# Inverse roots by a power, another order of a pair, an ending by batches, and a second copy loaded early

## The reference

```python
x = x + _layernorm(_L0_attn_ref(_layernorm(x), wq, bq, wkv, bkv, wo))
x = x + _layernorm(_L0_ffn_ref(_layernorm(x), gate_w, w_gate, w_up, w_down, sh_gate, sh_up, sh_down))
```

```python
scores = softmax(x @ gate_w.T);  topk_w, topk_idx = top_k(scores, 6)
# of 64 experts each takes the first 64 of its tokens; later ones are dropped
d = (silu(buf @ w_gate) * (buf @ w_up)) @ w_down       # per expert, 256 -> 176 -> 256
y = sum over the 6 of topk_w * d  +  (silu(x @ sh_gate.T) * (x @ sh_up.T)) @ sh_down.T
```

## Time and profile before

| | us |
|---|---|
| median of three runs | 1533.69 (1531.11 to 1537.27) |
| the profiled execution, whole | 1528.5 |
| its span, first to last instruction | 1526.7 |
| attention stage, about | 20 to 1262 |
| norms, router and picks of batch 7 | 1262 to 1307 |
| experts, first matmul to last scatter's landing | 1330.6 to 1471.0 |
| ending | 1471.0 to 1526.7 |

### The profile page before, as it was taken

The page is one execution under the profiler, slowest core; times in us unless marked ns, Lnnn a source line. Parts: engine busy times, 40 slices in busy tenths (PEclk is TensorE's granted clock), DMA queues, the critical chain, the costliest instruction groups (busy, mean ns, idle before and its releaser), DMA issues. The chain is left out here.

```text
span 1526.7 us, 26086 instructions
## 1 busy us (share of the span) xinstructions
PE 1374.1 (90%) x8451; PEld 1175.1 (77%) x8451; DVE 1117.0 (73%) x3622; ACT 855.1 (56%) x2299; POOL 814.1 (53%) x1309
## 2 busy tenths in 40 slices
PE   4899999999999999999999999999999994499930
PEld 3788889888988898988888898889888983355510
DVE  4867686889687968887788778977887776444427
ACT  4666666566656665666666666665666651144414
POOL 2556565546555655475546555655555541355546
PEclk9799999999999999999999999999999996799965
DMA  7100000100010001000100010001000057199963
GB/s 271 56 1 1 14 15 8 32 22 15 8 32 22 15 1 39 22 15 2 39 22 15 1 39 22 15 1 39 22 15 1 25 163 230 49 280 300 291 191 161
DMA packets 49462, 95.89 MB, mean 63 GB/s; under 512 B 4177, under 2 KB 36402, under 8 KB 49330
## 3 DMA queue, kind: packets, MB, share of 16 engines
q1 hardware_dynamic: 43186, 84.80, 16.6%
q0 software_dynamic: 6144, 9.44, 3.1%
HBM read 67.74 MB, written 26.48 MB: 62 GB/s over the span
## 5 line engine op out<-in xcount | busy, mean ns | idle before, releaser
L1524 POOL TENSOR_TENSOR prob<-prob,rinv 128x512 f32<-128x512 f32 (+3 forms) x512 | 366.9, 724 | 205.7 <-DVE rinv L1184 203.7
L879 ACT ACTIVATE prob<-prob,negmax 128x512 f32<-128x512 f32 (+3 forms) x512 | 285.4, 558 | 86.7 <-DVE negmax L1177 85.9
L1511 POOL TENSOR_TENSOR q_l<-q_sum,q_h 128x128 fp32r<-128x128 f32 (+1 forms) x256 | 185.4, 745 | 144.2 <-ACT q_h L859 143.1
L529 PE MATMUL bank_o<-pt_h,v_h 128*128 128x128 f32 (+3 forms) x512 | 169.2, 330 | 0.0
L529 PE MATMUL bank_o<-pt_h,v_l 128*128 128x128 f32 (+3 forms) x512 | 165.4, 323 | 0.0
L529 PE MATMUL bank_o<-pt_l,v_h 128*128 128x128 f32 (+3 forms) x512 | 164.0, 320 | 0.0
L888 ACT ACTIVATE pt_h<-bank_s 128x128 fp32r<-128x128 f32 (+3 forms) x214 | 92.9, 434 | 77.5 <-PE bank_s L609 58.9
L859 ACT ACTIVATE q_h<-q_sum 128x512 fp32r<-128x512 f32 x128 | 80.2, 626 | 90.1 <-DVE q_sum L1154 90.1
L1177 DVE CUSTOM_DVE_ANT_0 prob<-bank_t,causal 128x384 f32<-128x384 f32 (+3 forms) x226 | 110.4, 488 | 23.8 <-PE bank_t L529 22.9
L1177 DVE CUSTOM_DVE_ANT_0 prob<-bank_s,causal 128x512 f32<-128x512 f32 (+3 forms) x217 | 107.9, 497 | 24.9 <-PE bank_s L529 24.1
L529 PE MATMUL bank_y<-o_h,wo_h 128*128 128x512 f32 x256 | 112.1, 438 | 5.5 <-DVE o_l L1195 5.5
(11 more groups left out here) (365 smaller groups left out, 4170.6 us busy)
## 6 DMA issues: line engine op xcount, KB each, us to landing
w_gu<-in_w_in SPq DMA_DIRECT2D x32, 704.0 KB
w_dn<-in_w_out SPq DMA_DIRECT2D x32, 352.0 KB
xio<-in_x SPq DMA_DIRECT2D x16, 512.0 KB, 3.9
token_table<-rows SPq DMA_DIRECT2D x8, 640.0 KB, 3.7
ffn_sums<-keys SPq DMA_DIRECT2D x4, 1024.0 KB
x_rows<-xio SPq DMA_DIRECT2D x8, 512.0 KB, 2.9
ffn_sums<-ytr SPq DMA_DIRECT2D x16, 256.0 KB, 2.1
fx<-x_rows SPq DMA_DIRECT2D x8, 512.0 KB, 9.3
```

Source lines behind the costliest of these rows:

```text
L529: return pe.matmul(o, l, r, start=start, stop=stop, skip_group_check=True)
L879: act.activation(p_, p_, ACT.Exp, bias=negmax[:, r, i:i + 1], scale=-1.0, accum_out=rsum[:, r, i:i + 1]).then_inc(exp_made, 1)
L1511: pool.tensor_tensor(l_[:, cols], q_sum[:, cols], plain(h_)[:, cols], ALU.subtract).then_inc(pos_low, 1)
L1524: pool.tensor_tensor(p_, p_, rinv[:, r, i:i + 1].to_broadcast([P, (i + 1) * P]), ALU.mult).then_inc(prob_made, 1)
```

## The change

- **Power.** `newton` and the guess go. GpSimd adds EPS to the variances and raises them to -0.5 in one `pow` instruction: `inverse_root`, two instructions for 128x4 numbers. `QUIET` has one step for each norm.
- **Order of a pair.** On TensorE: `expert_in` of the next pair, `activations_turn`, `expert_turn`, `add_second` of the pair before, `expert_out`. ScalarE's order follows.
- **Ending by batches.** Statistics, power, bias (now one VectorE instruction), normalising and residual go one batch at a time; the last batch in two halves.
- **Copies.** `TAIL = 3`: pairs 29, 30 and 31 add to copy 0. Copy 1 is complete with pair 27, and its eight loads are issued as soon as that has landed; copy 0 is loaded after all scatters.

```diff
+        COPY = [j % 2 for j in range(NP - TAIL)] + [0] * TAIL
+        def scattered(j):
+            return 16 * COPY[:j + 1].count(COPY[j])
...
-            for i in range(2):
-                sp.wait_ge(dma_s[i], 16 * (NP // 2))
-            for b in range(NB):
-                load_sums(b)
+            sp.wait_ge(dma_s[1], 16 * COPY.count(1))
+            for b in range(NB):
+                sp.wait_ge(down_in, min(NP, LASTUSE[b]))
+                sp.dma_start(fb[b][:], sum_runs[1][b]).then_inc(dma_f[b], 16)
+            sp.wait_ge(dma_s[0], 16 * COPY.count(0))
+            for b in range(NB):
+                sp.dma_start(fa[b][:], sum_runs[0][b]).then_inc(dma_f[b], 16)
...
             for j in range(NP):
+                if j + 1 < NP:
+                    expert_in(j + 1)
+                activations_turn(j)
                 if j + 2 < NP:
                     expert_turn(j + 2)
                 if j:
                     add_second(j - 1)
-                activations_turn(j)
-                if j + 1 < NP:
-                    expert_in(j + 1)
                 expert_out(j)
...
+            for b in range(NB):
+                add_sums(b)
+                if b:
+                    bias(b - 1)
+                variances(b)
+                if b:
+                    residual_out(b - 1)
+            bias(LAST)
+            residual_out(LAST, 2)
...
+            def inverse_root(mvt, nwt, n):
+                variances[0] += 1
+                pool.wait_ge(var_made, variances[0])
+                y = nwt[:, 0, 0:n]
+                done(pool.tensor_scalar(y, mvt[:, 0:n, 1:2].rearrange("p i o -> p (i o)"), EPS, None, ALU.add))
+                pool.tensor_tensor(y, y, minus_half[:, 0:n], ALU.pow).then_inc(inv_made, 1)
...
             def scatter(j):
                 if j > 1:
-                    pool.wait_ge(dma_s[j % 2], 16 * (j // 2))
+                    pool.wait_ge(dma_s[COPY[j]], scattered(j) - 16)
...
+            for b in range(NB):
+                add_sums(b)
+                inverse_root(fmv[b % 2], fnw[b], TT)
```

More of the change, by code:

```diff
@@ L18 @@
 EPS = 1e-5
-MAGIC = 0x5F3759DF
 BIG = 3.0e38
@@ L46, in build @@
     TRASH = 2 * CAP
+    TAIL = 3
     SUMROWS = NT + TRASH
@@ L139, in build @@
         mv = place("mv", [P, TT, 2], F32)
-        nw = place("nw", [P, 4, TT], F32)
+        nw = place("nw", [P, 1, TT], F32)
+        minus_half = place("minus_half", [P, TT], F32)
         zero_f = keys[:, CAP:CAP + ROW]
@@ L1050, in scalar_program @@
             for j in range(NP):
+                if j + 1 < NP:
+                    expert_act(j + 1)
+                activations_turn(j)
                 if j + 2 < NP:
@@ L1054, in scalar_program @@
                     first_out(j - 1)
-                activations_turn(j)
-                if j + 1 < NP:
-                    expert_act(j + 1)
                 expert_out(j)
@@ L1092, in variance @@
                     last = dve.bn_aggr(mvt[:, i, :], statt[:, i, :])
-                done(last)
-                v, y, a = (nwt[:, q, 0:n] for q in range(3))
-                done(dve.tensor_scalar(v, mvt[:, 0:n, 1:2].rearrange("p i o -> p (i o)"), EPS, None, ALU.add))
-                done(dve.tensor_scalar(a.bitcast(I32), v.bitcast(I32), 1, None, ALU.logical_shift_right))
-                dve.tensor_scalar(y.bitcast(I32), a.bitcast(I32), -1.0, float(MAGIC), ALU.mult, ALU.add
-                                  ).then_inc(var_made, 1)
+                last.then_inc(var_made, 1)
             VARS = [("x", 0)]
@@ L1490, in done @@
                 pool.wait_ge(pool_step, steps[0])
-            def newton(nwt, n, r):
-                v, y, a = (nwt[:, q, 0:n] for q in range(3))
-                if r == 0:
-                    variances[0] += 1
-                    pool.wait_ge(var_made, variances[0])
-                done(pool.tensor_tensor(a, y, y, ALU.mult))
-                done(pool.tensor_tensor(a, a, v, ALU.mult))
-                done(pool.tensor_scalar(a, a, -0.5, 1.5, ALU.mult, ALU.add))
-                last = pool.tensor_tensor(y, a, y, ALU.mult)
-                if r < 2:
-                    done(last)
-                else:
-                    last.then_inc(inv_made, 1)
             def position(l_, h_, step):
@@ L1557, in gpsimd_program @@
             pool.memset(zero_f, 0.0).then_inc(zero_made, 1)
-            for r in range(3):
-                newton(nw, TT, r)
+            done(pool.memset(minus_half[:], -0.5))
+            inverse_root(mv, nw, TT)
             pool.wait_ge(consts_made, 1)
@@ L1663, in _, with shape_constants @@
             tensor_program(e)
-def shape_constants(T, d, NT, cap):
+def shape_constants(T, d, NT, cap, pairs=32, last=3):
     import numpy as np
@@ L1678, in shape_constants @@
     keys = np.broadcast_to(-np.arange(half, dtype=np.float32), (d, half))
-    copy_of = (np.arange(d) // 2 % 2 * (NT + 2 * cap)).astype(np.float32)
+    pair = np.arange(d) // 2
+    copy_of = np.where(pair < pairs - last, pair % 2 * (NT + 2 * cap), 0).astype(np.float32)
     copy_at = np.stack([copy_of, copy_of + NT], axis=1).astype(np.float32)
```

103 lines of the change are left out of this document (41 added, 62 removed).

## The result

The changed kernel takes **1512.96 us** (median of 4 runs, 1510.01 to 1516.31) against 1532.4 us of the kernel before in the same comparison (1529.34 to 1537.27). The profiled run of after is the slowest of its four; its span is 1514.3 us, 12.4 less than before's 1526.7. The forecast counted in spans too, and had 1525.8.

The account below looks back on a forecast made before the run. It took TensorE to bound the attention stage and scatters most of the expert stage. Start -1.0, open norms -6.4, order 0, scatters +6.0, ending +0.5 gave -0.9: span 1525.8, median 1532.8 us, range 1522 to 1543.

Parts of the forecast that it names:

- The 21 norms beside the heads cost nothing and give nothing: Attention stage: TensorE busy 1079.20 of 1090.00 us, so shortening the norms there was counted as 0.
- The lock: Ending: VectorE and GpSimd instructions exclude each other, making a cycle 5.6 + p = 6.0 us a batch.
- Open norms: Two norms where other engines wait: from aggregate to normalising 0.80 instead of 4.00 us, saving 6.4 us.
- p: Time of GpSimd's one power instruction at a norm, taken as 0.4 us.
- The start: First norm of all: VectorE reaches the normalising 1.5 us sooner, of which 1.0 us was counted as saved.
- Rival B: Power is dear: ten times on the chain, each us above 0.4 costs 10; 1543.7 at p = 1.5; chance 0.15.
- F + 56.2: Ending: forecast end of the span, counted from F, the issue of copy 0's loads; before F + 55.7, so +0.5 us.
- Order of a pair: Expert stage: 3.8 us a pair on TensorE instead of 4.13, but scatters set the pace, so 0 counted.
- Serial scatters beside loads: Expert stage's tail: last scatters one behind the other, slowed by 4 MB of loads; last landing 1477.0 against 1471.0, +6.0 us.
- Rival A: Expert stage's tail: scatters not slowed by the loads, +0.4 in place of +6.0 us, total 1527.2; chance 0.18.
- The shorter load buys nothing: Ending: the chain of additions and statistics takes the place of the shorter load, +0.5 us.
- rival D: Ending: no lock between VectorE and GpSimd, cycle 4.4 us, six of them 9.6 less, total 1523.2; chance 0.12.

Follow-up runs that it names:

- e1_guess: Changed kernel with VectorE's three small guess steps put back at every norm but the ending's, results unused: 1516.18 us (0.990 of the kernel before).
- e5_newton: Changed kernel with eight of Newton's twelve small GpSimd steps put back, results unused, addition and power behind them: 1530.58 us (1.000 of the kernel before).
- e2_order: Changed kernel with the old order of a pair's pieces on TensorE and ScalarE: 1513.19 us (0.987 of the kernel before).
- e6_order: Kernel before with the power and the new order of a pair, nothing else of the change: 1492.58 us (0.975 of the kernel before).
- e8_ahead: Changed kernel with the ending's additions one batch ahead of the statistics and the bias on GpSimd: 1504.32 us (0.982 of the kernel before).
- e10_after: Changed kernel, unchanged, profiled once more: 1522.59 us.

## Why the prediction was wrong, step by step

The forecast of 1532.8 was 19.8 us too high. Of these, 11.5 lie in the spans (1525.8 forecast, 1514.3 measured). The other 8.3 come of which runs were profiled: that of before was 5.2 us below its median, which the forecast added, and that of after 3.4 above its own.

- **"The 21 norms beside the heads cost nothing and give nothing" failed.** It put at nothing what gave 19.2 us in the six batches alone, more than the whole 11.5; the middle of the expert stage hid a part of it. It was an argument from TensorE's busy time: 1079.20 of 1090.00 left 10.8 us. But busy time hid two things: the gaps are larger in the weight loads than in the matmuls (0.53 against 0.33 us at 370.45), and what counts is matmuls per us. The Trainium skill says in "Perfetto Trace Analysis", section "Identifying the Most-Contended Engine", that matmul busy time is no good measure of how near the limit TensorE is, and has one look at the busy share of weight loads and at what the matmuls compute instead. The trace agrees: busy time rose 1.0%, weight loads 1.9%, matmuls done 2.05%. The rows that should have been asked for are the waits of TensorE's weight loads: 15.3 us in six batches, each on a VectorE instruction. Experiments e1_guess and e5_newton show the norms' small steps to be their cause: VectorE's guess 0.9 us a batch, GpSimd's Newton the rest.
- **The lock was known and used in one place only.** Rows 10 gave it, in the form needed: the 1.68 us are those of a VectorE instruction with one tensor as input, as the normalising is. (The prediction set them beside a rule on instructions with two inputs; of its two rows only the 1.11 is of that kind.) The same row-by-row look at VectorE's normalising (516 and 614 ns in the middle, where the same form takes 399 at the least) would have shown VectorE losing some 2.4 us a batch.
- **Open norms: mechanism right, size off.** 2 x 2.53 = 5.1 us instead of 6.4, since p is 1.04, not 0.4. The small step of 0.20 was no guide to it. The start gave 1.4, of 1.0 forecast.
- **Rival B fell though its power was dear.** At p = 1.04 its rule gave 6.4 us more, of which 1.3 came, at the open norms. The ending's cycle came out at 6.06 all the same, since VectorE's addition (0.42) runs under the power, where the sum had put one behind the other. That F + 56.75 stood against F + 56.2 is therefore luck: a power taken too short and an addition that costs nothing cancelled. (The sum's last stretch, from GpSimd's start of batch 7 on, also makes 11.2 + p by its own terms, not 11.0 + p.)
- **Order of a pair: right for this kernel.** The scatters held (28 of 32 waited), and e2_order gives the same time. The reason reached too far: it denied a gain at the end of the stage too, and with alternating copies that is 3.6 us of tail (e6_order).
- **Serial scatters beside loads: +6.0 forecast, +5.1 in the profiles.** Within it pair 29 took longer and pair 30 less than forecast. Measured against what the new order allows (12.1) rather than against before (15.7), the tail costs 8.8 us in the profiles, 5.1 of it the loads'. Rival A falls.
- **"The shorter load buys nothing" held within 1.5 us** (56.75 against 58.1 and 58.25 with both copies loaded late), and so did the two-sided lock of the ending, but for VectorE's addition beside the power; rival D falls as a whole, though e8_ahead shows that 10 us lay in the order of the steps and the place of the bias. What the sum never asked was what the old closing would do with the power: 47.5 to 47.9 us, 9 less than the new one.
- **The middle of the expert stage, 0 forecast, +9.3 in the first profiles.** The forecast said "scatters in the middle still 8 to 9 us to landing" and TensorE's "share there lower": the share is lower (42.06 of 50 us instead of 47.77), the landings are longer (9.6). Its cause is open, as said above. The line drawn for "wrong altogether" (an end sooner than 140 us after the first matmul) was not crossed: from first scatter to last landing alone the stage got longer, 131.8 to 146.2 us, and the kernel is faster in spite of it. None of the signs that the prediction listed lies in the attention stage, so none could have shown the step that failed.

## What to carry to other kernels

When an engine looks full, list its waits and count its instructions per us before writing "nothing to gain there"; follow each wait to what stands ahead of the releaser on its own engine. Small steps on GpSimd have a price that shows on VectorE: compare the middle with the least duration of one and the same VectorE instruction. And of a change in several parts, time the parts: here the power gave 34 us and the order another 3 to 5, and the copies and the closing took about 20 back.

## What was not expected of the hardware

- GpSimd's power of 128 x 4 numbers takes 1.04 us, of 128 x 8 1.68, so about 0.4 fixed and 0.16 a column; the small addition beside it 0.23.
- VectorE's normalising of 128 x 256 (one tensor and two numbers a partition as inputs) takes 0.40 us at the least and up to 1.11; at the place read, four of them took 2.37 us beside GpSimd's two-input subtraction, and 1.46 without it.
- TensorE's clock fell to the lower level for 20 us in the midst of the expert stage in one run (e10_after), behind a stretch with 3.4 us idle in 20; in another run of the same kernel a stretch with as much idle time was followed by the full clock.
- One kernel's two profiles differ by 6 us in one stage (125.4 and 131.7) at equal times everywhere ahead of it (pitch 151.6 in both).
